# Another order of tasks, maxima items and delays in a fused attention and gated FFN kernel

## The chip, the cores and the metric

The kernel runs on one core of a Trainium2 chip. The metric is the device time of one launch in microseconds, as the median of three runs. The program is one long list of instructions for each engine: TensorE (PE in the profile), VectorE (DVE), ScalarE (ACT), GpSimd (POOL) and SyncE (SP), which here only issues DMAs. Each engine runs its own list strictly in order and waits on semaphores for the others.

## What is computed

```python
xn = layernorm(x)                      # x: (8, 1024, 256)
q, k, v = split(xn @ W_attn + b_attn)  # 16 heads of 16, rope over the heads' axis
att = softmax(causal(q @ k.T / 4))     # per batch and head, 1024 x 1024
s = (att @ v) @ W_proj + b_proj
g = silu((silu(xn @ wg.T) * (xn @ wu.T)) @ wd.T)   # 768 hidden, integer weights / 127
out = x + s * g
```

The tables of the rotation are made for 16 rows and applied along the axis that holds the heads.

## The kernel before

The eight batches run one after the other. The program has a prologue, a body `first` for batch 0, six bodies `mid`, a body `last` and an epilogue. A body has 36 steps (the code says slots): 4 groups of 4 heads, 9 steps each. A step has two halves, a and b. In a half TensorE computes the scores of two heads for one part of the causal triangle (L876, into the three PSUM banks `st`); ScalarE takes the exponential of them (L1133, into `pexp`); GpSimd sets the part above the diagonal to zero in the blocks that touch it (L1618, called the mask here); one step later, in half b, TensorE multiplies `pexp` with the values into `acc` (L927).

The softmax needs the maximum of each row before the exponential. It is computed 12 steps ahead from a second product of the same queries and keys (L903) into the ring, four more PSUM banks, and VectorE reduces it: this is a maxima item. Each half of a step has one item of a kind A, B, E or F out of the table `ITEMS`, two ring banks each. An F item is two plain reductions of 512 columns (L1304). The others touch the diagonal and are masked on the way (L1300): E is one piece of 512 columns a bank, A pieces of 384 and 128, B two pieces of 256. The step that stands at a multiple of nine plus n uses the entry of `ITEMS` that is three further on, so the first entry of the table serves steps 6, 15, 24 and 33.

All other work hangs in these steps as tasks, by the table `TASKS`, which is written out in the code. The names: TX turns the normalised x, QK makes queries and keys, V values, UPG and UPU are the two sides of the FFN's hidden layer, DN its down product, FP the output projection, MT turns the maxima; each of these takes one ring bank. LNS, LNR and LNA are the statistics, the reciprocal roots and the normalising of the layernorm of the next batch; XC copies half of its columns. YS moves unnormalised outputs, YG gathers the sums, YR takes their reciprocal on VectorE, YB stores it, YC spreads it, YN multiplies with it and splits (YH, YL). `("UPU", 1, 3)` is the fourth of six blocks of the second half of the tokens.

TensorE runs a step as: scores, maxima item a, the tasks in the order of the table, scores, maxima item b, the values product. The ring banks are given out in turn in exactly that order, and a use waits until the bank's use four before it is freed. ScalarE and VectorE do the tasks of a half sorted by kind, as `parts_at` lists them (ScalarE: TX, QK, UPG, UPU, V, DN, FP, MT; VectorE: TX, QK, UPG, DN, LNS, MT), not in the table's order. A table `LAG` says how many halves after its step an engine's part of a task stands in that engine's list. SP stores and loads q and k through DRAM; `load_x` brings the x of the batch after the next.

Of the kernel before, what the change touches and what calls it, by code (L numbers as in the profile page):

```python
# [80 lines left out]


TASKS = {
    0: [("DN", 1, 2), ("YS", 3, 0), ("YS", 3, 1)],
    1: [("XC", 0), ("UPG", 0, 0)],
    2: [("V", 0, 1), ("LNS", 0)],
    3: [("XC", 1), ("YG", 1), ("DN", 1, 3)],
    4: [("YR", 1), ("LNS", 1), ("UPG", 0, 1), ("UPU", 0, 0)],
    5: [("LNS", 2), ("UPU", 0, 1), ("YB", 1), ("YC", 1), ("V", 1, 1), ("LNS", 3)],
    6: [("LNR",), ("V", 1, 0)],  # L90
    7: [("UPG", 0, 2), ("YN", 1, 0), ("MT", 1), ("YS", 0, 0), ("YN", 1, 1)],
    8: [("UPU", 0, 2)],
    9: [("LNA", 1), ("UPG", 0, 3)],
    10: [("UPU", 0, 3), ("LNA", 2)],
    11: [("LNA", 5), ("UPG", 0, 4)],
    12: [("FP", 0)],
    13: [("UPU", 0, 4)],
    14: [("YS", 0, 1), ("UPG", 0, 5), ("UPU", 0, 5)],
    15: [("LNA", 6), ("LNA", 3), ("FP", 1), ("LNA", 7), ("FP", 2), ("LNA", 4), ("LNA", 0)],
    16: [("UPG", 1, 0), ("MT", 2)],  # L100
    17: [("YS", 1, 0), ("TX", 0, 1), ("TX", 0, 0), ("TX", 1, 1), ("UPG", 1, 1)],
    18: [("DN", 0, 0)],
    19: [("YS", 1, 1), ("TX", 1, 0), ("QK", 0, 1, 1), ("DN", 0, 1)],
    20: [("DN", 0, 2), ("QK", 0, 0, 1), ("YG", 0), ("QK", 0, 0, 0), ("QK", 0, 1, 0)],
    21: [("DN", 0, 3)],
    22: [("YR", 0), ("UPU", 1, 0), ("UPU", 1, 1)],
    23: [("UPG", 1, 2)],
    24: [("YB", 0), ("QK", 1, 1, 0), ("YC", 0), ("UPU", 1, 2)],
    25: [("FP", 3), ("MT", 3)],
    26: [("UPG", 1, 3), ("UPU", 1, 3)],  # L110
    27: [("YS", 2, 0), ("YN", 0, 0), ("UPG", 1, 4)],
    28: [("YS", 2, 1), ("UPU", 1, 4)],
    29: [("UPG", 1, 5)],
    30: [("YN", 0, 1), ("UPU", 1, 5)],
    31: [("QK", 1, 1, 1), ("QK", 1, 0, 0)],
    32: [("QK", 1, 0, 1)],
    33: [("DN", 1, 0), ("DN", 1, 1)],
    34: [("MT", 0)],
    35: [("V", 0, 0)],
}  # L120
# [1707 lines left out]
```

How the kernel before makes its waits and increments, by code:

```python
def wait(eng, sem, count):  # L375
    if isinstance(count, int) and count <= 0:
        return
    eng.wait_ge(sem, count)
# [183 lines left out]
        def turn(eng, we, wo, cos, sin, tmp, chain, base=0, scale=None):  # L563
            for dst, a, b in ((tmp[0], we, cos), (tmp[1], wo, sin), (tmp[2], wo, cos), (tmp[3], we, sin)):
                if scale is None:
                    last = eng.tensor_tensor(dst, a, b, ALU.mult)
                else:
                    last = eng.scalar_tensor_tensor(out=dst, in0=a, scalar=scale, in1=b, op0=ALU.mult, op1=ALU.mult)
            last.then_inc(chain, 1)
            eng.wait_ge(chain, base + 1)
            eng.tensor_tensor(we, tmp[0], tmp[1], ALU.subtract)
            return eng.tensor_tensor(wo, tmp[2], tmp[3], ALU.add)
# [12 lines left out]
        def rstd_steps(eng, kind, i, pause):  # L586
            base = LN_EACH * ln_number(kind, i) + 2 * TT
            def step(ins, k):
                ins.then_inc(ln_chain, 1)
                if k < 2 + 4 * NEWTON:
                    eng.wait_ge(ln_chain, base + k)
                    if pause is not None:
                        stand(eng, pause)
            eng.wait_ge(ln_chain, base)
            if pause is not None:
                stand(eng, pause)
            step(eng.tensor_scalar(lne[:, :], lnv[:, :, 1], EPS, None, ALU.add), 1)
# [15 lines left out]
        def wait_ready(eng, kind, i, task, name=""):  # L616
            eng.wait_ge(ring_ready[bank(kind, task, name)], use(kind, i, task, name))
```

## Time and profile before

| | |
|---|---|
| median of 3 runs | 1210.34 us (1209.96 to 1210.91) |
| the profiled execution | 1210.59 us |
| its span, first to last instruction | 1208.6 us |
| TensorE, VectorE, ScalarE, GpSimd busy | 93%, 84%, 73%, 63% |
| mean granted clock of TensorE | 0.992 |

The span is what the rows below are counted in; 2 us of the time lie outside it. A duration in a row holds the time until the result is written, so the rows of an engine that never waits overlap; the distance of two starts tells what an instruction takes from its engine. A bracket at a row's end is idle time ahead of it and what ended it.

### The profile page before, as it was taken

The page shows a single profiled execution, that of the slowest core. Times are in us where ns is not written, and L with a number is a line of the kernel's source. Part 1 is how long each engine was busy: PE and PEld are TensorE (multiplying, and loading weights), DVE is VectorE, ACT ScalarE, POOL GpSimd, SP SyncE. Part 2 cuts the span into 40 slices and gives each one's busy share as a digit, 9 for nine tenths or more (in the row PEclk, how much of TensorE's full clock was granted, in tenths as well). Part 3 has the DMA queues.
Part 4 walks back from the last instruction along what each step waited for, and adds up shares of the span by engine and source line. Part 5 has one row for each costly group of instructions (what it writes and reads, how often), then busy time and mean ns, then how long its engine had stood idle before and what let it go on. Part 6 is the DMA issues. An engine that isn't in the chain of part 4 may idle for free.

```text
span 1208.6 us, 27562 instructions
## 1 busy us (share of the span) xinstructions
PE 1125.6 (93%) x9484; PEld 454.8 (38%) x9484; DVE 1012.8 (84%) x3100; ACT 886.5 (73%) x1700; POOL 761.9 (63%) x934
## 2 busy tenths in 40 slices
PE   3789999999999999999999999999999999999996
PEld 2323333434343343434334343343434343343433
DVE  6989989988989888988799878898898887989822
ACT  3358777777877768777777768777787776878774
POOL 3237545495846949298564967469492894747672
PEclk9979999999999999999999999999999999999999
DMA  6250052312442151511624025321525114240201
GB/s 176 71 153 11 11 160 75 88 29 96 105 119 53 30 161 46 137 30 50 165 72 100 20 84 122 120 52 30 144 66 139 30 33 147 72 97 15 62 2 53
DMA packets 69359, 97.49 MB, mean 81 GB/s; under 512 B 16478, under 2 KB 42468, under 8 KB 69220
## 3 DMA queue, kind: packets, MB, share of 16 engines
q1 hardware_dynamic: 69182, 95.72, 29.0%
q8 instruction: 75, 1.23, 0.4%
q14 instruction: 64, 0.52, 0.2%
q10 hardware_dynamic: 38, 0.01, 0.0%
HBM read 52.76 MB, written 34.47 MB: 72 GB/s over the span
## 4 chain that ended last, share of the span: by engine, by line
PE 55%; POOL 20%; DVE 11%; ACT 7%; issue 6%; DMA 1%; POOLq 0%; SPq 0%; DVEq 0%; ACTq 0%
PE ring L936 27%; PE acc L927 12%; PE st L876 8%; PE ring L903 6%; POOL xn L583 5%; POOL hf L1648 4%; DVE ring L1300 3%; POOL pexp L1618 3%; ACT pexp L1133 3%; POOL hT L1657 2%; DVE mx_s L1304 2%; POOL hT L1652 1%; POOL yn L1667 1%; PE ring L946 1%; ACT parts L1175 1%
## 5 line engine op out<-in xcount | busy, mean ns | idle before, releaser
L1133 ACT ACTIVATE pexp<-st 128x512 f32<-128x512 f32 x1152 | 623.7, 598 | 132.1 <-PE st L876 129.6
L1300 DVE CUSTOM_DVE_ANT_0 ring<-ring,tri 128x512 f32<-128x512 f32 (+3 forms) x1024 | 470.6, 522 | 37.3 <-PE ring L903 36.5
L1618 POOL TENSOR_SCALAR_AFFINE_SELECT pexp<-pexp 128x512 f32<-128x512 f32 x256 | 158.0, 635 | 336.2 <-ACT pexp L1133 245.6
L1304 DVE TENSOR_REDUCE mx_s<-ring 128x1 f32<-128x512 f32 x512 | 326.2, 681 | 30.6 <-PE ring L903 29.2
L927 PE MATMUL acc<-pexp,v_pad 128*17 128x512 f32 (+3 forms) x3072 | 304.1, 490 | 16.4 <-POOL pexp L1618 13.8
L903 PE MATMUL ring<-k_st,q_st 56*128 56x512 f16 (+4 forms) x1536 | 239.3, 326 | 17.4 <-DVE g L1372 11.0
L876 PE MATMUL st<-q_st,k_st 58*128 58x512 f16 (+3 forms) x1536 | 234.3, 331 | 3.9 <-ACT pexp L1133 3.4
L876 PEld LDWEIGHTS st<-q_st,k_st 58*128 58x128 f16 x1536 | 61.8, 93 | 276.3 <-ACT pexp L1133 184.3
L1300 DVE DVE_READ_ACCUMULATOR2_ANT mx_s<- 128x1 f32 x1024 | 144.8, 141 | 0.0
L1648 POOL TENSOR_TENSOR hf<-ga,ups 128x512 f32<-128x512 f32 x96 | 121.9, 1274 | 6.9 <-DVE ga L1364 5.3
L927 PEld LDWEIGHTS acc<-pexp,v_pad 128*17 128x17 f32 x3072 | 61.5, 96 | 152.5 <-issue 119.4
L1657 POOL TENSOR_TENSOR hT<-hf,hT 128x512 f16<-128x512 f32 x96 | 111.0, 1160 | 6.7
L903 PEld LDWEIGHTS ring<-k_st,q_st 56*128 56x128 f16 (+1 forms) x1536 | 82.1, 95 | 65.0 <-DVE g L1372 12.9
L936 PE MATMUL ring<-w_dn,hT 128*128 128x256 bf16 x768 | 93.3, 273 | 2.6 <-DVE mx_s L1304 2.3
L936 PE MATMUL ring<-xh,w 128*128 128x512 f16 x256 | 85.1, 387 | 1.1 <-DVE mx_s L1304 0.2
L1364 DVE SCALAR_TENSOR_TENSOR ga<-th,ring 128x512 f32<-128x512 f32 x96 | 66.0, 687 | 19.9 <-ACT th L1190 18.1
L936 PEld LDWEIGHTS ring<-w_dn,hT 128*128 128x128 f16 x768 | 71.6, 98 | 28.6 <-issue 14.8
L1175 ACT ACTIVATE parts<-ring,b_qk 128x512 f16<-128x512 f32 x64 | 44.0, 687 | 45.1 <-PE ring L936 44.9
L936 PE MATMUL ring<-xh,w_ga 128*128 128x512 f16 x192 | 74.2, 386 | 0.7 <-DVE mx_s L1300 0.2
L936 PE MATMUL ring<-xh,w_up 128*128 128x512 f16 x192 | 73.4, 382 | 0.7
L936 PE MATMUL ring<-xl,w_ga 128*128 128x512 f16 x192 | 73.3, 382 | 0.0
L936 PE MATMUL ring<-xl,w_up 128*128 128x512 f16 x192 | 72.8, 379 | 0.0
(151 smaller groups left out, 1322.4 us busy)
## 6 DMA issues: line engine op xcount, KB each, us to landing
parts_scratch<-parts SPq DMA_DIRECT2D x32, 512.0 KB, 3.1
q_st<-parts_scratch SPq DMA_DIRECT2D x62, 192.0 KB, 3.8
k_st<-parts_scratch SPq DMA_DIRECT2D x62, 192.0 KB, 4.4
parts_scratch<-parts SPq DMA_DIRECT2D x32, 256.0 KB, 3.6
xo<-in_x SPq DMA_DIRECT2D x32, 256.0 KB, 3.3
out<-xo SPq DMA_DIRECT2D x32, 256.0 KB, 2.3
xn<-in_x SPq DMA_DIRECT2D x7, 1024.0 KB, 8.0
yn<-yT SPq DMA_DIRECT2D x224, 32.0 KB
```

The lines of the kernel that those rows point to most:

```text
L583: eng.tensor_scalar(xn[:, tt, :], xn[:, tt, :], lnv[:, tt, 0:1], rstd[:, tt:tt + 1], ALU.subtract, ALU.mult).then_inc(xn_ready, 1)
L876: mm = nc.tensor.matmul(st[:, (GH * n + 2 * p + a) % NST, at:at + w], k_st[rows, g, p, kb * P:(kb + 1) * P], q_st[rows, g, p, q0:q0 + w], ...
L903: mm = nc.tensor.matmul(dst[:, at:at + w], q_st[rows, g, p, t * P:(t + 1) * P], k_st[rows, g, p, k0:k0 + w], start=k == 0, stop=k == len(f ...
L927: mm = nc.tensor.matmul(acc[32 * j:32 * j + D + 1, CH - w:CH], v_pad[:, kb, GH * g + j, :], pexp[:, GH * (m % NSET) + j, at:at + w], start ...
L936: mm = nc.tensor.matmul(dst, left, right, start=k == 0, stop=k == len(pairs) - 1)
L1133: nc.scalar.activation(pexp[:, GH * (n % NSET) + j, :], st[:, (GH * n + j) % NST, :], ACT.Exp, scale=1.0 / (QK_SCALE * np.sqrt(D))).then_i ...
L1300: top_ = nc.vector.tensor_tensor_reduce(out=src, in0=src, in1=tri[:, CH - w:CH], scale=1.0, scalar=NEG, op0=ALU.add, op1=ALU.max, accum_ou ...
L1304: top_ = nc.vector.reduce_max(dst, src, AX.X)
L1364: nc.vector.scalar_tensor_tensor(out=ga[:, t[2] % 2, :], in0=th[:, th_buffer(kind, t), :], scalar=1.0, in1=src, op0=ALU.add, op1=ALU.mult) ...
L1618: nc.gpsimd.affine_select(out=t, in_=t, compare_op=ALU.is_ge, fill=0.0, base=0, pattern=[[0, GH], [1, P]], channel_multiplier=-1).then_inc ...
L1648: nc.gpsimd.tensor_tensor(hf[:, u, :], ga[:, u, :], ups[:, u, :], ALU.mult).then_inc(h_full, 1)
L1657: nc.gpsimd.tensor_tensor(hT[:, 1, m, :], hf[:, m % 2, :], hT[:, 0, m, :], ALU.subtract)\
```

## The change

The tables `TASKS`, `ITEMS` and the parts of `LAG` for GpSimd and SP are replaced, and `load_x` stands in step 28 of a body, not in step 21. No instruction is added or removed, and ScalarE's and VectorE's delays stay. A few lines of the diff:

```diff
-ITEMS = ('BF', 'EA', 'FF', 'FF', 'AE', 'AF', 'EA', 'EF', 'BF')
+ITEMS = ('AF', 'FF', 'EF', 'AE', 'FE', 'AF', 'BF', 'EB', 'AF')
...
-    20: [("DN", 0, 2), ("QK", 0, 0, 1), ("YG", 0), ("QK", 0, 0, 0), ("QK", 0, 1, 0)],
+    20: [("QK", 0, 1, 0), ("QK", 0, 0, 0), ("DN", 0, 2)],
...
-LOAD_X = [slot for slot in TASKS if TX_LAST in TASKS[slot]][0] + 2
+LOAD_X = 28
...
-    "gpsimd": {"LNR": 2, "LNA": 0, "XC": 1, "UPU": 2, "HI": 4, "LO": 4, "FP": 2, "FP_G": 2, "FP_X": 4, "YN": 1, "YH": 1, "YL": 2},
-    "sync": {"QK": 2, "MT": 0, "FP": 5, "YS": 0, "YG": 0, "YB": 0, "YC": 1},
+    "gpsimd": {"LNR": 2, "LNA": 0, "XC": 0, "UPU": 3, "HI": 4, "LO": 5, "FP": 2, "FP_G": 3, "FP_X": 5, "YN": 1, "YH": 1, "YL": 4},
+    "sync": {"QK": 6, "MT": 2, "FP": 5, "YS": 2, "YG": 1, "YB": 1, "YC": 3},
```

The tasks of a middle batch that lie on TensorE, by step, before: 0 DN; 1 UPG; 2 V; 3 DN; 4 UPG UPU; 5 UPU V; 6 V; 7 UPG MT; 8 UPU; 9 UPG; 10 UPU; 11 UPG; 12 FP; 13 UPU; 14 UPG UPU; 15 FP FP; 16 UPG MT; 17 TX TX TX UPG; 18 DN; 19 TX QK DN; 20 DN QK QK QK; 21 DN; 22 UPU UPU; 23 UPG; 24 QK UPU; 25 FP MT; 26 UPG UPU; 27 UPG; 28 UPU; 29 UPG; 30 UPU; 31 QK QK; 32 QK; 33 DN DN; 34 MT; 35 V. Now: 0 none; 1 DN; 2 V; 3 DN; 4 UPG UPU; 5 UPG UPU V; 6 V; 7 UPG MT; 8 to 16 as before; 17 TX TX UPG; 18 QK DN; 19 TX TX QK DN; 20 QK QK DN; 21 DN; 22 UPU; 23 UPG UPU; 24 QK UPU; 25 UPG MT; 26 FP; 27 UPU; 28 UPG UPU; 29 UPG; 30 QK UPU; 31 QK; 32 QK; 33 DN; 34 DN MT; 35 V. LNA stand in steps 9, 10, 11 and five times in 15; now in 10, 11, twice in 14, three times in 15, and in 17.

TensorE, step 20 of the fourth batch, from its first maxima to its second, before (L903 are maxima, w_dn is DN, w16 with xh and xl is QK, L876 are scores):

```order
L903 MATMUL ring<-k_st,q_st 128x384 x2
L903 MATMUL ring<-k_st,q_st 128x128 x2
L936 MATMUL ring<-w_dn,hT 128x256 x12
L936 MATMUL ring<-xh,w16 128x512
L936 MATMUL ring<-xl,w16 128x512
L936 MATMUL ring<-xh,w16 128x512 x2
```

and the same place now, with the line numbers of the changed file, one lower:

```order
L935 MATMUL ring<-xl,w16 128x512
L935 MATMUL ring<-xh,w16 128x512
L935 MATMUL ring<-w_dn,hT 128x256 x12
L875 MATMUL st<-q_st,k_st 128x256 x4
L902 MATMUL ring<-k_st,q_st 128x512 x2
```

DN has gone from before the QK tasks to behind them, next to the scores. VectorE's list at this place, before:

```order
L1355 SCALAR_TENSOR_TENSOR parts<-ring,b_qk,parts 128x512 x3
L1372 SCALAR_TENSOR_TENSOR g2<-th,ring 128x256
L1304 TENSOR_REDUCE mx_s<-ring 128x1 x2
```

and now:

```order
L1354 SCALAR_TENSOR_TENSOR parts<-ring,b_qk,parts 128x512 x2
L1371 SCALAR_TENSOR_TENSOR g2<-th,ring 128x256
L1303 TENSOR_REDUCE mx_s<-ring 128x1 x2
```

Here the QK parts stand before DN's g2 in both, with one QK less now. GpSimd from the end of the rstd chain of LNR to the masks of steps 10 and 11, before (yn and ynT are YN, YH and YL, hf and hT are UPU and its halves, xn is LNA):

```order
L608 TENSOR_TENSOR rstd<-rstd,lnt 128x8
L1667 TENSOR_TENSOR yn<-yn 128x512 x2
L1673 CAST ynT<-yn 128x512 x2
L1676 TENSOR_TENSOR ynT<-yn,ynT 128x512 x2
L1648 TENSOR_TENSOR hf<-ga,ups 128x512
L583 TENSOR_SCALAR xn<-xn,lnv,rstd 128x256
L1618 AFFINE_SELECT pexp<-pexp 128x4x128
L1652 CAST hT<-hf 128x512
L1657 TENSOR_TENSOR hT<-hf,hT 128x512
L583 TENSOR_SCALAR xn<-xn,lnv,rstd 128x256
L1618 AFFINE_SELECT pexp<-pexp 128x4x128 x2
```

and now:

```order
L607 TENSOR_TENSOR rstd<-rstd,lnt 128x8
L1656 TENSOR_TENSOR hT<-hf,hT 128x512
L1666 TENSOR_TENSOR yn<-yn 128x512 x2
L1672 CAST ynT<-yn 128x512 x2
L1675 TENSOR_TENSOR ynT<-yn,ynT 128x512 x2
L1647 TENSOR_TENSOR hf<-ga,ups 128x512
L1617 AFFINE_SELECT pexp<-pexp 128x4x128
L1651 CAST hT<-hf 128x512
L582 TENSOR_SCALAR xn<-xn,lnv,rstd 128x256
L1656 TENSOR_TENSOR hT<-hf,hT 128x512
L1617 AFFINE_SELECT pexp<-pexp 128x4x128 x2
```

The LNA ahead of the first mask is gone, and one low part of UPU has come behind the chain from in front of it.

## Rows read from the trace of the kernel before

**Rows 1.** The page: its head, and the busy time of each engine.
```profile
span 1208.6 us, 27562 instructions
...
PE 1125.6 (93%) x9484; PEld 454.8 (38%) x9484; DVE 1012.8 (84%) x3100; ACT 886.5 (73%) x1700; POOL 761.9 (63%) x934
```
**Rows 2.** Windows: stretch, length, busy time and count of each engine, clock, DMA.
```profile
78.00:84.00 6.00, 6.00 (x35) 1.43 (x33) 5.53 (x17) 3.63 (x7) 2.34 (x4) 0.57 1.02 291
...
495.47:637.38 141.91, 135.98 (x1176) 54.70 (x1173) 123.19 (x379) 108.18 (x209) 96.05 (x116) 1.00 0.31 85
```
**Rows 3.** Timeline of PE in step 20: start, length, line, tiles, idle time before.
```profile
578.81 0.38 PE L936 MATMUL ring<-xh,w 128*128 128x512 f16 x1
579.12 0.39 PE L876 MATMUL st<-q_st,k_st 58*128 58x256 f16 x4
581.09 0.39 PE L903 MATMUL ring<-k_st,q_st 56*128 56x512 f16 x2 [1.57 <-DVE g L1372]
```
**Rows 4.** Timeline of DVE in step 20.
```profile
580.62 0.41 DVE L1372 SCALAR_TENSOR_TENSOR g<-th,ring 128x256 f32<-128x256 f32 x1
```
**Rows 5.** Timeline of PE in steps 10 and 11.
```profile
533.68 0.57 PE L903 MATMUL ring<-k_st,q_st 56*128 56x512 f16 x2
535.34 0.62 PE L927 MATMUL acc<-pexp,v_pad 128*17 128x512 f32 x4 [1.09 <-POOL pexp L1618]
...
538.06 0.38 PE L903 MATMUL ring<-k_st,q_st 56*128 56x512 f16 x2
539.54 0.94 PE L927 MATMUL acc<-pexp,v_pad 128*17 128x384 f32 x10 [1.09 <-POOL pexp L1618]
```
**Rows 6.** Timeline of POOL, the rstd chain's start and the mask of step 10.
```profile
521.17 0.25 POOL L600 TENSOR_SCALAR lne<-lnv 128x8 f32<-128x8 f32 x1
...
534.64 0.64 POOL L1618 TENSOR_SCALAR_AFFINE_SELECT pexp<-pexp 128x512 f32<-128x512 f32 x1
```
**Rows 7.** Timeline of POOL and PE, steps 15 to 17.
```profile
554.85 6.03 POOL L583 TENSOR_SCALAR xn<-xn,lnv,rstd 128x256 f32<-128x256 f32 x5
...
560.13 0.63 PE L946 MATMUL ring<-ident,xn 128*128 128x128 f32 x4
560.93 1.14 PE L946 MATMUL ring<-ident,xn 128*128 128x128 f32 x8 [0.17 <-POOL xn L583]
```
**Rows 8.** Timeline of PE in step 34, half b.
```profile
631.87 0.77 PE L876 MATMUL st<-q_st,k_st 58*128 58x512 f16 x2
...
632.89 1.05 PE L927 MATMUL acc<-pexp,v_pad 128*17 128x512 f32 x8
```
**Rows 9.** Timeline of PE and DVE in step 6.
```profile
518.29 0.38 PE L903 MATMUL ring<-k_st,q_st 56*128 56x256 f16 x4
519.36 0.29 PE L936 MATMUL ring<-w,xh 128*128 128x128 f16 x2 [0.69 <-DVE mx_s L1304]
...
518.64 1.26 DVE L1304 TENSOR_REDUCE mx_s<-ring 128x1 f32<-128x512 f32 x2
```
**Rows 10.** Groups by form, 495.47 to 637.38: count, busy us, mean ns, idle before.
```profile
L1304 DVE TENSOR_REDUCE mx_s<-ring 128x1 f32<-128x512 f32 x65 | 41.5, 681 | 4.2 <-PE ring L903 4.1
...
L1300 DVE CUSTOM_DVE_ANT_0 ring<-ring,tri 128x384 f32<-128x384 f32 x32 | 18.5, 579 | 1.7 <-PE ring L903 1.7
```
**Rows 11.** Timeline of SP's queue, steps 22 to 25.
```profile
589.77 0.40 SPq L689 DMA_DIRECT2D xn<-in_x  x1
...
598.08 4.79 SPq L756 DMA_DIRECT2D yn<-inv_scratch  x8
```
**Rows 12.** DMA issues: count, KB each, median us from issue to landing.
```profile
xn<-in_x SPq DMA_DIRECT2D x7, 1024.0 KB, 8.0
...
ysum<-sums_scratch SPq DMA_DIRECT2D x14, 32.0 KB, 2.9
```
**Rows 13.** Timeline of SP's queue and DVE, steps 3 and 5.
```profile
507.06 0.34 SPq L742 DMA_DIRECT2D ysum<-sums_scratch  x1
...
514.62 0.55 DVE L1340 RECIPROCAL yinv<-ysum 128x64 f32<-128x64 f32 x1
```

More of the change, by code:

```diff
@@ L83 @@
 TASKS = {
[L84 to L91, printed above, removed]
+    1: [("DN", 1, 2)],
+    2: [("YS", 3, 0), ("XC", 0), ("XC", 1), ("V", 0, 1), ("LNS", 0), ("YS", 3, 1)],
@@ L92 @@
+    3: [("DN", 1, 3)],
+    4: [("LNS", 1), ("UPG", 0, 0), ("YG", 1), ("YR", 1), ("UPU", 0, 0)],
+    5: [("UPG", 0, 1), ("LNS", 2), ("LNS", 3), ("UPU", 0, 1), ("YB", 1), ("YC", 1), ("V", 1, 0)],
+    6: [("LNR",), ("V", 1, 1)],
+    7: [("UPG", 0, 2), ("YN", 1, 0), ("YN", 1, 1), ("MT", 1)],
     8: [("UPU", 0, 2)],
-    9: [("LNA", 1), ("UPG", 0, 3)],
-    10: [("UPU", 0, 3), ("LNA", 2)],
-    11: [("LNA", 5), ("UPG", 0, 4)],
+    9: [("UPG", 0, 3), ("YS", 0, 0)],
+    10: [("LNA", 7), ("UPU", 0, 3)],
@@ L96 @@
+    11: [("UPG", 0, 4), ("YS", 0, 1), ("LNA", 4)],
     12: [("FP", 0)],
-    13: [("UPU", 0, 4)],
-    14: [("YS", 0, 1), ("UPG", 0, 5), ("UPU", 0, 5)],
-    15: [("LNA", 6), ("LNA", 3), ("FP", 1), ("LNA", 7), ("FP", 2), ("LNA", 4), ("LNA", 0)],
+    13: [("UPU", 0, 4), ("YS", 1, 0)],
+    14: [("UPG", 0, 5), ("LNA", 5), ("UPU", 0, 5), ("LNA", 0)],
+    15: [("FP", 1), ("LNA", 6), ("FP", 2), ("LNA", 1), ("LNA", 2)],
     16: [("UPG", 1, 0), ("MT", 2)],
-    17: [("YS", 1, 0), ("TX", 0, 1), ("TX", 0, 0), ("TX", 1, 1), ("UPG", 1, 1)],
@@ L102 @@
-    18: [("DN", 0, 0)],
-    19: [("YS", 1, 1), ("TX", 1, 0), ("QK", 0, 1, 1), ("DN", 0, 1)],
-    20: [("DN", 0, 2), ("QK", 0, 0, 1), ("YG", 0), ("QK", 0, 0, 0), ("QK", 0, 1, 0)],
[4 rows of a table added]
     21: [("DN", 0, 3)],
[L106 to L112, printed above, removed]
@@ L113 @@
-    29: [("UPG", 1, 5)],
[L114 to L118, printed above, removed]
[1 row of a table added]
+    23: [("UPG", 1, 2), ("UPU", 1, 1)],
+    24: [("YB", 0), ("YC", 0), ("QK", 1, 1, 0), ("UPU", 1, 2)],
+    25: [("UPG", 1, 3), ("MT", 3)],
+    26: [("YN", 0, 0), ("FP", 3)],
+    27: [("UPU", 1, 3)],
+    28: [("UPG", 1, 4), ("UPU", 1, 4)],
+    29: [("UPG", 1, 5)],
[5 rows of a table added]
     35: [("V", 0, 0)],
```

9 rows, old and new, of the table TASKS are left out of this document.

## The prediction

> **What bounds the kernel now.** I read the page first: TensorE is busy 93% of the span, VectorE 84%, the rest less [rows 1]. TensorE's clock is granted in full in the middle batches and falls to 0.57 for some us near the start [rows 2]. That share does not show how much room is left, because the rows give every matmul a modelled tail: matmuls of 512 columns follow each other every 0.22 us while each is listed with 0.38 [rows 3]. So I cut the span at the first score matmul of each batch. One of the six middle batches lasts 141.9 us [rows 2], the other five 141.6 to 142.1; together they are 851 of the 1208.6 us. Then I went through TensorE's rows of the batch that starts at 495.47 and compared each start with the start before it and with the same pair of kinds elsewhere. Scores are followed by their maxima after 0.23 us, maxima by the values product after 0.31. What is longer than that is waiting. Summed over a batch it is about 10 us, so a batch without any wait would take about 131 us. What ended each wait stands in the brackets of its row. The large ones stand at the same places in each middle batch:
>
> - Step 20: the second maxima start at 581.09, 1.97 us after the scores at 579.12, where 0.23 is natural: **1.74 us** [rows 3]. The reason is an order. TensorE runs DN 0 2 before three QK tasks, while ScalarE and VectorE serve QK before DN in a half step. Ring banks are used in turn, four of them: MX, MX, DN, QK, QK, QK, MX. The last needs DN's bank, and VectorE empties that one last, with g at 580.62, after its third QK [rows 4].
> - Steps 10 and 11: the values product waits for the masked pexp: 1.66 and 1.48 us where 0.31 is natural, so **1.35 and 1.17** [rows 5]. GpSimd is late there: from the rstd chain at 521.17 it works without a pause, two YN with their YH and YL, one UPU, one LNA, and comes to the mask at 534.64 [rows 6]. Two more waits of about 0.15 follow in steps 12 and 13, 2.8 us in all.
> - Step 17: the TX tasks wait for GpSimd's five LNA in a row, 6.03 us from 554.85: 0.10 us at 560.13 and 0.36 at 560.93 (four transposes take 0.44), **0.5 us** [rows 7].
> - Step 34: step 34 has almost no TensorE work and an E and an A item for VectorE. Scores at 631.87 to values at 632.89 is 1.02 us for 0.54: **0.5 us** [rows 8].
> - Step 6: V 1 0 waits **0.8 us** (518.29 to 519.36 is 1.07, 0.31 natural) for a bank that VectorE empties late, after two LNS parts; its reductions come at 518.64 [rows 9].
>
> **The change, part by part.** All instructions stay; the count of tasks and items per batch is equal. So the sum is one of waits.
>
> *Step 20.* The step now runs QK, QK, DN, in the order in which ScalarE and VectorE serve them. I went through every step with several tasks: nowhere does TensorE's order now disagree with theirs. The whole 1.74 us goes in the first batch and the six middle ones, since all have these tasks (the last has not): 7 x 1.74 = 12.2 us. One QK has moved to step 18; it takes 1.3 us of TensorE (six matmuls at 0.22), no burst.
>
> *Steps 10 to 13.* Ahead of the mask of step 10 GpSimd now has one LNA less, 1.2 us (five take 6.03 [rows 7]), and the low part of UPU 0 1 has changed places with the rstd chain; both stand ahead of the mask as before, so that is worth nothing. If GpSimd's list of steps 5 to 10 starts when it did, the first wait falls from 1.35 to 0.15. It may start up to 1 us earlier, for steps 0 and 1 have lost an UPG and TensorE comes to step 5 sooner; or UPG 0 1, now one step later, may feed it late and eat the 1.2. Later masks have the same work between them as before. So of 2.8 us between 0.5 and 1.7 stay, at worst all; I take 0.9 and a gain of 1.9 for six batches: 11.4 us. In the first batch there is no YN, and little to gain.
>
> *Step 17.* LNA 5 and 0 stand in step 14, three in 15, LNA 3 in 17, and the two TX tasks that read it in step 19. The first two TX have their inputs 2 us ahead. LNA 3 ends about when TX 0 0 wants it (GpSimd's work up to it ends near 73 us of the batch, TensorE is there near 73), so I keep 0.1 of 0.5: 7 x 0.4 = 2.8 us.
>
> *Step 34 and items.* DN 1 1 comes in front of MT 0 and the items are F and F. VectorE needs about 3.1 us (two F items are four reductions, about 0.6 us each by the pair that takes 1.26 with its tail [rows 9], plus the two tasks) against 3.1 of TensorE: the 0.5 goes, less 0.1: 7 x 0.4 = 2.8 us. Steps 7 and 16 get F, F for E, A as well; their small waits of 0.3 in sum give about 0.3 x 6 = 1.8.
>
> *Step 0* has no TensorE task now. Entering full-height matmuls from the row-split ones costs 0.31 instead of 0.22 us (578.81 to 579.12 [rows 3]), twice a step: 0.2 x 7 = 1.3 us.
>
> *What it costs.* An A item takes VectorE about 1.5 us, F 1.2, E 1.3, B 1.5 (estimates from the means of F's and A's rows and their like [rows 10], less the 0.1 by which such rows overlap). Steps 0 to 5 give VectorE 16.2 us of items where it had 16.0, and step 0 pairs 2.8 us of VectorE with 1.7 of TensorE. VectorE is the last to finish there already (the wait at step 6). I add 0.3 us x 7 = 2. For new short waits elsewhere (UPG 1 1 behind UPU 0 5, V at step 29 behind a mask that comes later, TX 0 0) I set 0.5 x 6 = 3; from below nothing, from above 1.5 a batch.
>
> *x two batches ahead from step 28.* The 1 MB load used to stand before the 32 KB store of inverses: it is issued at 589.77, the store 0.7 us later, and the spreads that wait for that store are issued only at 598.08 [rows 11]. Afterwards the spread comes about 5 us earlier. On the end it is worth nothing: GpSimd reaches YN later anyway, and the scores of step 27, whose row of maxima is queued behind the spreads, hardly wait. The load needs 8 us [rows 12] and is read from step 2 on, over 30 us later: covered. SP's delays of 6 for QK and 2 or 3 for YS, MT, YC do not hold it: SP stands still for data only, and the two stacks of step 24 are issued as soon as QK is done.
>
> Sum: -12.2 -11.4 -2.8 -2.8 -1.8 -1.3 + 2 + 3 = -27.3. The profiled execution took 1210.59 us, 2 more than its span, and 0.25 above the median of the runs: 1210.59 - 27.3 = 1183.3, **1183 us**.
>
> **Rivals.**
> - *Only step 20 pays.* Every wait removed elsewhere gives GpSimd and VectorE less time, and they are busy 96 and 123 of its 142 us [rows 2]; VectorE's list in steps 0 to 6 is full. For it: the wait at step 6 stays. Against: the masks' lateness is a matter of what stands before them. It gives 1210.6 - 12.2 = 1198.
> - *The gather blocks VectorE: slower.* Now all eight stack loads, the two xo loads and both YS stand in front of YG in SP's queue, and YG and the reciprocal YR are in the same half step 4b; VectorE waits in line on it with all maxima behind. Before, the gather was issued at 507.06, 7.6 us before the reciprocal at 514.62 [rows 13]; it lands after 2.9 us [rows 12], which leaves 4.7 us. If YG is issued over 4.7 us later, each further us is one of VectorE and of TensorE behind it. The moves of y are small and now queue behind eight loads of the stacks. At 4.7 us plus the 4.5 us that a middle batch gains, so from YG 9 us late, it decides; 10 us late, 5.3 over for six batches, gives 1183 + 32 = 1215. Against: the stack loads only change places with YS 3 1, which waits for step 1. The Trainium skill's page "DMA: Bandwidth & Descriptors", section "Queues, rings and completion order", says that descriptors are taken in ring order on each DMA engine, which speaks for this rival. By that rule a late YG follows, and the trace agrees in the inverse store behind the x load.
> - *More than I count.* All of steps 10 to 17 and half of step 6 go: 5 us more over six batches and more in the first, whose start runs at that lower clock for some us [rows 2]: 1163 to 1173.
> - *Nothing.* The waits move on to VectorE's late maxima: 1210.
>
> **How the numbers follow.** The forecast's own range: downward no new waits (-5), 0.5 us kept at the masks (-2.4) and none in steps 17 and 34 (-2.1), 1173; upward 1.7 us kept (+4.8) and 1.5 us a batch of new waits (+6), 1194. It has 0.70. More: 0.08. Only step 20: 0.12. Nothing: 0.04. Slower: 0.06. The range takes in the forecast, half of the case above it in gain and the step-20 case with 5 us of spread: 1168 to 1203. The rest, some 0.18, is out. A measurement here tells 0.2%, 2.4 us, from no change. Faster 0.89 (the first three, less a little), same 0.04, slower 0.07.
>
> **What would show it.** Middle batches of about 137.4 us. In step 20 the second maxima 0.23 us after the scores. The wait of the values product for masks in steps 10 and 11 under 1 us in sum, the mask of step 10 about 38.0 to 39 us after the batch's start (it was 39.2). No wait at TX in step 17. The wait at V in step 6 still 0.7 to 0.9. The reciprocal with no idle time before it. It is wrong if VectorE idles at L1339, if the order in SP's queue delays the stacks for step 24 or the row of maxima for step 0, or if waits for VectorE's maxima grow by over 3 us a batch.

## The result, and the profile after

The changed kernel takes 1180.2 us (median of 4, 1179.2 to 1180.5) where the kernel before, timed beside it, takes 1210.6 (1209.96 to 1211.26). The ratio is 0.9747, 95% interval 0.9730 to 0.9764. The forecast was 1183 with a range of 1168 to 1203: 27.3 us off were forecast and 30.4 came.

The page of the kernel after, its head and the busy time of each engine:

```profile
span 1177.2 us, 27562 instructions
...
PE 1119.9 (95%) x9484; PEld 454.4 (39%) x9484; DVE 1011.4 (86%) x3100; ACT 886.4 (75%) x1700; POOL 761.5 (65%) x934
```

The work is the same, instruction for instruction, and so is VectorE's and GpSimd's busy time [rows 1]; only the span is 31.4 us shorter. The fourth and the third batch, each cut from its first score matmul to the next batch's:

```profile
484.32:621.94 137.62, 135.25 (x1177) 54.65 (x1174) 123.25 (x379) 108.15 (x209) 96.03 (x116) 1.00 0.31 87
346.23:484.32 138.09, 135.05 (x1177) 54.58 (x1174) 123.09 (x379) 108.16 (x209) 96.11 (x116) 1.00 0.32 87
```

The other four middle batches last 136.1 to 137.2 (before: 141.6 to 142.1 each [rows 2]); these two are the longest: the third waits 1.7 us at step 24, the fourth 0.4 there and 0.9 more in steps 27 to 29. Step 24 is taken up below. By place, from the same cuts in both traces: prologue +0.8, first batch -2.8, six middle batches 850.7 to 821.8, so -28.8, last batch and epilogue -0.6; the sum is -31.4.

The waits, place by place. For every pair of consecutive groups on TensorE (scores, maxima, values, tasks) I took the usual shortest distance of such a pair in the trace before, and called what is longer a wait. The mean per middle batch, in us, by steps; small entries up to about 0.2 are also differences between shapes. The kernels below the second line are those of the experiments. A pair that the trace before does not have is not counted; one such pair, maxima to values in step 31, is long in e15_qk2, so its entry for steps 30 to 33 is that of the changed kernel, 0.53, and the 4.64 us that these steps last longer (19.79 for 15.15). Where TensorE's clock falls behind a wait, the slower matmuls are in the numbers too.

```
run               0    1-4    5-6    7-9  10-13  14-16     17  18-19     20  21-23     24  25-29  30-33  34-35  total
before         0.07   0.94   0.85   0.51   3.01   0.38   0.65   0.19   1.78   0.25   0.31   0.42   0.53   0.56  10.46
after          0.70   0.15   1.04   0.28   0.66   0.26   0.40   0.21   0.04   0.10   0.59   0.49   0.53   0.08   5.53
e1_step20      0.07   0.94   0.85   0.51   3.01   0.38   0.66   0.19   0.05   0.24   0.31   0.59   0.53   0.56   8.88
e2_dn_first    0.70   0.15   1.03   0.29   0.67   0.26   0.41   0.20   1.78   0.10   0.22   0.52   0.53   0.08   6.94
e6_one_lna     0.07   0.93   0.85   0.51   1.79   0.38   1.63   0.21   1.78   0.24   0.31   0.42   0.53   0.56  10.21
e9_lna_and_tx  0.07   0.93   0.85   0.51   1.80   0.38   0.50   5.01   1.78   0.24   0.30   0.36   0.53   0.56  13.84
e12 (+ delays) 0.07   0.95   0.85   0.51   1.60   0.38   0.49   1.00   1.79   0.25   0.30   0.36   0.64   0.56   9.76
e5g_pool_lag   0.70   0.15   1.04   0.28   0.87   0.26   0.40   3.49   0.04   0.10   0.10   0.50   0.53   0.08   8.56
e15_qk2        0.70   0.15   1.03   0.28   0.66   0.26   0.40   0.21   0.04   7.27   1.59   0.33   5.17   0.08  18.17
e4_load21      0.70   0.15   1.04   0.28   0.67   0.26   0.40   0.20   0.04   0.10   3.01   0.41   0.53   0.08   7.88
e7_items       0.71   0.30   0.65   0.51   0.97   0.38   0.50   0.39   0.04   0.46   0.24   0.51   0.53   0.08   6.26
e14_dn0        0.07   1.35   1.04   0.28   0.66   0.26   0.40   0.21   0.04   0.10   0.55   0.50   0.53   0.08   6.07
```

Two places carry most of the gain, 1.7 us in step 20 and 2.35 in steps 10 to 13. Step 20 in the timeline of PE after, which answers to [rows 3]:

```profile
565.13 0.39 PE L875 MATMUL st<-q_st,k_st 58*128 58x256 f16 x4
565.36 0.38 PE L902 MATMUL ring<-k_st,q_st 56*128 56x512 f16 x2
```

The second maxima stand 0.23 us behind the scores, where 1.97 lay before, and have no bracket. Step 11, where the values product waited for the mask [rows 5]:

```profile
525.35 0.38 PE L902 MATMUL ring<-k_st,q_st 56*128 56x512 f16 x2
525.80 1.06 PE L926 MATMUL acc<-pexp,v_pad 128*17 128x384 f32 x16
```

The distance is 0.45 us where 0.31 is natural, 0.14 of wait for 1.17; in step 10 it is 0.07 for 1.35. The timelines of POOL and PE in the same batch, the mask of step 10 and LNA 3, and the TX of step 19 that reads it:

```profile
521.02 0.64 POOL L1617 TENSOR_SCALAR_AFFINE_SELECT pexp<-pexp 128x512 f32<-128x512 f32 x1
...
553.77 1.22 POOL L582 TENSOR_SCALAR xn<-xn,lnv,rstd 128x256 f32<-128x256 f32 x1
```
```profile
555.42 1.09 PE L945 MATMUL ring<-ident,xn 128*128 128x128 f32 x8
```

The mask of step 10 comes 36.7 us after the batch's start (521.02 less 484.32), earlier than the 38 to 39 forecast; it was 39.2 [rows 2, 6]. LNA 3 ends at 554.99, only 0.4 us before its TX starts. That narrow margin is the key to the experiments below.

### The profile page after: what moved, and what is told of

Read it like the earlier page. It is cut to its first block, busy times and chain, and to the rows that moved or that the text cites. A ratio compares the mean times of both kernels' runs of the same rounds, so it can differ in the third digit from the quotient of the medians.

```text
span 1177.2 us, 27562 instructions
## 1 busy us (share of the span) xinstructions
PE 1119.9 (95%) x9484; PEld 454.4 (39%) x9484; DVE 1011.4 (86%) x3100; ACT 886.4 (75%) x1700; POOL 761.5 (65%) x934
## 4 chain that ended last, share of the span: by engine, by line
PE 60%; POOL 14%; DVE 8%; issue 6%; DMA 5%; ACT 4%; SPq 2%; POOLq 0%; DVEq 0%; ACTq 0%
PE ring L935 26%; PE acc L926 15%; PE st L875 10%; PE ring L902 7%; POOL xn L582 3%; DVE ring L1299 2%; POOL hf L1647 2%; ACT pexp L1132 2%; POOL pexp L1617 2%; DVE mx_s L1303 1%; DMA k_st<-parts_scratch 1%; POOL yn L1666 1%; DMA parts_scratch<-parts 1%; POOL so L1686 1%; POOL hT L1656 1%
## 5 line engine op out<-in xcount | busy, mean ns | idle before, releaser
L902 PE MATMUL ring<-k_st,q_st 56*128 56x512 f16 (+5 forms) x1536 | 235.9, 326 | 9.5 <-ACT ups L1180 3.3
L935 PE MATMUL ring<-xh,w 128*128 128x512 f16 x256 | 87.7, 388 | 0.3
```

The source lines that it names most:

```text
L902: mm = nc.tensor.matmul(dst[:, at:at + w], q_st[rows, g, p, t * P:(t + 1) * P], k_st[rows, g, p, k0:k0 + w], start=k == 0, stop=k == len(f ...
L935: mm = nc.tensor.matmul(dst, left, right, start=k == 0, stop=k == len(pairs) - 1)
```

## The experiments

Each was timed in five rounds beside the kernel before, which took 1209.7 to 1210.4 us. The changed kernel's 1180.2 is the other end of the scale. Each says what it is an edit of.

**Step 20 alone** (an edit of the kernel before):

```diff
-    20: [("DN", 0, 2), ("QK", 0, 0, 1), ("YG", 0), ("QK", 0, 0, 0), ("QK", 0, 1, 0)],
+    20: [("QK", 0, 0, 1), ("YG", 0), ("QK", 0, 0, 0), ("QK", 0, 1, 0), ("DN", 0, 2)],
```

> The kernel before with one edit: in step 20 DN 0 2 stands last, behind the three QK tasks; nothing is moved between steps. The prediction's term: the 1.74 us of step 20 goes in seven batches, 12.2 us, so about 1198.4, ratio 0.990, and the second maxima start 0.23 us after the scores. Rival (the wait moves): DN's hand-over comes later in the half step, VectorE's last hand-over is then late for the first maxima of step 21 or for the value product behind it, and less than half is kept: 1204 to 1210.

Measured: 1198.9 us, ratio 0.9902 (0.9885 to 0.9919). Its step 20 in the timeline of PE:

```profile
573.27 0.39 PE L876 MATMUL st<-q_st,k_st 58*128 58x256 f16 x4
573.50 0.38 PE L903 MATMUL ring<-k_st,q_st 56*128 56x512 f16 x2
```

The distance is 0.23, the whole wait of 1.7 us is gone (table, column 20), and hardly anything comes up elsewhere: 11.4 us of the 12.2. The order within one step is shown to be the cause, and the wait does not move on.

**The same the other way** (an edit of the changed kernel):

```diff
-    20: [("QK", 0, 1, 0), ("QK", 0, 0, 0), ("DN", 0, 2)],
+    20: [("DN", 0, 2), ("QK", 0, 1, 0), ("QK", 0, 0, 0)],
```

> The changed kernel with DN 0 2 first in step 20 again, ahead of its two QK tasks. Four ring banks are used in turn, so the second of the two maxima groups of half b needs DN's bank, which VectorE empties last. If the order is what counts, a wait of 1 to 1.7 us is back there in seven batches: 1187 to 1192. Rival (three QK tasks in one step were the trouble, and the one moved to step 18 is what helped): under 0.3 us a batch, 1180 to 1182.

Measured: 1187.6 us, ratio 0.9813 (0.9795 to 0.9831), 7.4 more than the changed kernel. The timeline of PE, first and second head of the second maxima, which are two uses of the ring here:

```profile
570.27 0.38 PE L902 MATMUL ring<-k_st,q_st 56*128 56x512 f16 x1
572.00 0.39 PE L902 MATMUL ring<-k_st,q_st 56*128 56x512 f16 x1 [1.35 <-DVE g L1371]
```

With one QK less in the step the second head's use still falls on DN's bank, and waits for the same g. In the trace the wait is 1.7 again, and 0.4 comes back at step 24, whose loads then have more time.

**One LNA moved behind the masks** (an edit of the kernel before):

```diff
-    9: [("LNA", 1), ("UPG", 0, 3)],
+    9: [("UPG", 0, 3)],
-    14: [("YS", 0, 1), ("UPG", 0, 5), ("UPU", 0, 5)],
+    14: [("YS", 0, 1), ("UPG", 0, 5), ("LNA", 1), ("UPU", 0, 5)],
```

> The kernel before with one edit: LNA 1 stands in step 14 and not in step 9, so GpSimd has 1.2 us less to do ahead of the masks of steps 10 and 11, and as much more between them and the TX tasks of step 17. The prediction's account of the masks (their lateness is only a matter of what stands ahead of them): the wait of step 10 falls by 1.2 us in six batches and the rest stays, 7.2 us, about 1203.4. Rival (GpSimd has no pause between the masks of step 4 and the last LNA, so its work up to the first TX task sets the time of step 17, wherever it stands): the mask wait falls by 1.2 us, the wait at TX in step 17 grows from 0.5 to about 1.7, and the time is 1210.5, within 1.5.

Measured: 1210.05 us, ratio 0.9997 (0.9986 to 1.0008): nothing. The timelines of PE, steps 11 and 17, and of POOL, the five LNA of step 15:

```profile
540.33 0.94 PE L927 MATMUL acc<-pexp,v_pad 128*17 128x384 f32 x10 [1.04 <-POOL pexp L1618]
...
561.65 0.66 PE L946 MATMUL ring<-ident,xn 128*128 128x128 f32 x4 [0.76 <-POOL xn L583]
562.85 1.09 PE L946 MATMUL ring<-ident,xn 128*128 128x128 f32 x8 [0.55 <-POOL xn L583]
```
```profile
556.76 6.04 POOL L583 TENSOR_SCALAR xn<-xn,lnv,rstd 128x256 f32<-128x256 f32 x5
```

Steps 10 to 13 lose 1.2 us of wait and step 17 gains 1.0: what the mask gives, TX takes back. GpSimd's timeline before has no idle time between the masks of step 4 at 513.57 and the last of the five LNA, but for the bubbles inside the rstd chain. So its whole list up to there is one block of about 47 us, and TensorE is held to it at the next point where it needs a result. The prediction's account of the masks by itself falls here.

**The places of LNA and TX taken over** (an edit of the kernel before; FP, YS and all others stay):

```diff
-    9: [("LNA", 1), ("UPG", 0, 3)],
-    10: [("UPU", 0, 3), ("LNA", 2)],
-    11: [("LNA", 5), ("UPG", 0, 4)],
+    9: [("UPG", 0, 3)],
+    10: [("LNA", 7), ("UPU", 0, 3)],
+    11: [("UPG", 0, 4), ("LNA", 4)],
-    14: [("YS", 0, 1), ("UPG", 0, 5), ("UPU", 0, 5)],
-    15: [("LNA", 6), ("LNA", 3), ("FP", 1), ("LNA", 7), ("FP", 2), ("LNA", 4), ("LNA", 0)],
+    14: [("YS", 0, 1), ("UPG", 0, 5), ("LNA", 5), ("UPU", 0, 5), ("LNA", 0)],
+    15: [("FP", 1), ("LNA", 6), ("FP", 2), ("LNA", 1), ("LNA", 2)],
-    17: [("YS", 1, 0), ("TX", 0, 1), ("TX", 0, 0), ("TX", 1, 1), ("UPG", 1, 1)],
+    17: [("YS", 1, 0), ("TX", 1, 1), ("LNA", 3), ("TX", 0, 1), ("UPG", 1, 1)],
-    19: [("YS", 1, 1), ("TX", 1, 0), ("QK", 0, 1, 1), ("DN", 0, 1)],
+    19: [("TX", 0, 0), ("YS", 1, 1), ("TX", 1, 0), ("QK", 0, 1, 1), ("DN", 0, 1)],
```

> The kernel before with the places of the eight LNA and of the TX tasks taken from the changed kernel: no LNA in step 9, LNA 7 and 4 in 10 and 11, 5 and 0 in 14, 6, 1 and 2 in 15, LNA 3 behind TX 1 1 in step 17, TX 0 0 in step 19; all else as before. By the prediction's terms it is worth 1.2 to 1.9 us at the masks and 0.4 at TX per batch: 9.6 to 14.2 us, 1196 to 1201. By the rival of the run with one LNA moved, the gain needs the TX tasks' later deadline and is that whole sum here and nothing there; TX in step 17 then has no wait, and the masks of steps 10 to 13 keep about 1.2 of 2.8 us, since two halves of UPU and YL still stand ahead of them. If only the order of the LNA within GpSimd's list counted, this run would gain no more than the run with one LNA moved.

Measured: 1229.4 us, ratio 1.0146 (1.0125 to 1.0167): 19 us slower than before, which neither theory had. The timelines of POOL and PE at steps 17 to 19, and the window behind the wait:

```profile
567.05 2.50 POOL L1687 TENSOR_TENSOR so<-so,b_pr 128x512 f32<-128x512 f32 x2
...
574.46 1.21 POOL L583 TENSOR_SCALAR xn<-xn,lnv,rstd 128x256 f32<-128x256 f32 x1
```
```profile
575.73 1.09 PE L946 MATMUL ring<-ident,xn 128*128 128x128 f32 x8 [3.22 <-POOL xn L583]
...
577.89 0.63 PE L936 MATMUL ring<-xl,w 128*128 128x512 f16 x1
578.32 0.63 PE L936 MATMUL ring<-xh,w 128*128 128x512 f16 x1
```
```profile
576.00:581.00 5.00, 5.00 (x26) 2.96 (x24) 2.04 (x3) 1.77 (x3) 0.27 (x1) 0.66 0.49 133
```

LNA 3 stands in GpSimd's list behind the whole of FP 1 and FP 2 (bias, gate and residual, six operations from 567.05 to 574.46, 7.4 us) and is late by 3.2 us for TX 0 0. Then the clock's granted share is 0.66 over the next 5 us: matmuls of 512 columns follow each other after 0.43 us in place of 0.22, the rate of the lower of the two levels. Both together are the 5.0 of column 18-19. The gain at the masks (1.2) is there again and is swallowed.

**The same with GpSimd's new delays**. The edit is the last one and

```diff
-    "gpsimd": {"LNR": 2, "LNA": 0, "XC": 1, "UPU": 2, "HI": 4, "LO": 4, "FP": 2, "FP_G": 2, "FP_X": 4, "YN": 1, "YH": 1, "YL": 2},
+    "gpsimd": {"LNR": 2, "LNA": 0, "XC": 0, "UPU": 3, "HI": 4, "LO": 5, "FP": 2, "FP_G": 3, "FP_X": 5, "YN": 1, "YH": 1, "YL": 4},
```

> The kernel before with the places of LNA and TX of the changed kernel (the run that came out at 1229) and with GpSimd's new row of delays as well. The 2.5 us of residual additions stand behind LNA 3 now, so that it ends near 72.0 us of the batch and not near 74.5, where TensorE comes to it near 71.3: the wait of 4.8 us of step 19 falls to about 0.7, 1.7 of it being the clock that no longer falls. With 1.2 us of the mask wait of step 10 gone as before: about 1204. Rival (the wait of step 19 has to do with the place of TX or QK on TensorE, not with GpSimd's list): it stays near 1229.

Measured: 1206.1 us, ratio 0.9974 (0.9963 to 0.9986), 23 less than without the delays. PE at step 19, where LNA 3 ends at 565.26:

```profile
564.83 0.38 PE L903 MATMUL ring<-k_st,q_st 56*128 56x384 f16 x4
565.32 1.09 PE L946 MATMUL ring<-ident,xn 128*128 128x128 f32 x8
```

TX waits 0.2 us (0.49 for 0.31), and 0.6 to 0.8 stand in step 18, where DN waits for its hT. The wait of step 19 was GpSimd's list, as the theory has it, and 1206 is close to the 1204 reckoned.

**GpSimd's delays taken out of the changed kernel**: the reverse of the last diff.

> The changed kernel with GpSimd's row of delays as it was before (UPU 2, LO 4, XC 1, FP_G 2, FP_X 4, YL 2), all else changed. Theory from the run with LNA and TX moved (GpSimd works without a pause from the masks of step 4 to LNA 3, and what stands ahead of LNA 3 sets when TX 0 0 of step 19 can start): FP_X at 4 puts both residual additions of FP 1 and 2 ahead of LNA 3, 2.5 us; LNA 3 ends 0.4 us ahead of its TX now, so TX waits about 2.1 us in the six middle batches, and up to 1.7 more where TensorE's clock falls after the wait: 1193 to 1203. Rival (the delays only say where things stand and are worth nothing, as the prediction took them to be): 1180, within 1.5.

Measured: 1197.8 us, ratio 0.9904 (0.9887 to 0.9921), 17.6 us more than the changed kernel. PE at step 19:

```profile
562.60 1.09 PE L945 MATMUL ring<-ident,xn 128*128 128x128 f32 x8 [2.08 <-POOL xn L582]
```

2.1 us, as reckoned from 2.5 of work and 0.4 of margin. In the six middle batches TensorE stands idle there for 1.9 to 2.2 us, and in four of them 1.5 to 1.7 us of slower matmuls come behind it. So GpSimd's row of delays carries more than the order in step 20. The run changes the whole row; the wait is of the size of the two additions of FP_X, which the row puts ahead of LNA 3, but FP_X was not tried by itself.

**SP's delays taken out of the changed kernel**:

```diff
-    "sync": {"QK": 6, "MT": 2, "FP": 5, "YS": 2, "YG": 1, "YB": 1, "YC": 3},
+    "sync": {"QK": 2, "MT": 0, "FP": 5, "YS": 0, "YG": 0, "YB": 0, "YC": 1},
```

> The changed kernel with SP's row of delays as it was before (QK 2, MT 0, YS 0, YG 0, YB 1, YC 1), all else changed. Theory: the waits of 0.3 to 1.7 us for the stacks at step 24 (in batches 2, 3, 5 and 6), of 0.5 at step 27 and 29 in batch 3, 4.3 us in all, come from QK's parts being stored 6 half steps late, close ahead of the loads that step 24 needs; with 2 they go: 1176. Rival (they come from the traffic on the DMA engines, or another transfer is late once QK's go first): 1179 to 1182, with the waits at other places.

Measured: 1271.8 us, ratio 1.0517 (1.0499 to 1.0536): 92 us slower than the changed kernel, where 4 faster was expected. (YB goes back to 0 in this run as well; the expectation has it as 1.) It was the largest miss of the study, and this run settled it:

**Only QK's delay on SP** (an edit of the changed kernel, `"QK": 6` to `"QK": 2`):

> The changed kernel with one number of SP's row put back, QK 2 in place of 6. Theory from the run with the whole row (1272): SP then issues the four stores of parts, waits for their receipt, issues eight loads, and only then comes to the gather YG; its sums land behind the place of the reciprocal, VectorE stands there for 6 us and TensorE behind it. That one number makes the whole loss: 1268 to 1275. Rival (YS, YC or YG in the row had a share): under 1250.

Measured: 1269.6 us, ratio 1.0490 (1.0471 to 1.0509). One number makes nearly all of it. SP's queue, VectorE, PE and windows, steps 20 to 24 of its fourth batch:

```profile
601.94 0.64 SPq L675 DMA_DIRECT2D parts_scratch<-parts  x1
607.13 0.80 SPq L636 DMA_DIRECT2D q_st<-parts_scratch  x2
...
610.89 0.35 SPq L741 DMA_DIRECT2D ysum<-sums_scratch  x1
```
```profile
617.39 0.55 DVE L1339 RECIPROCAL yinv<-ysum 128x64 f32<-128x64 f32 x1 [7.81 <-DMA ysum<-sums_scratch]
```
```profile
618.77 0.60 PE L902 MATMUL ring<-k_st,q_st 56*128 56x512 f16 x1 [6.68 <-DVE mx_s L1299]
```
```profile
615.00:618.00 3.00, 0.00 (x0) 0.00 (x0) 0.61 (x2) 0.00 (x0) 1.76 (x2) 0.58 0.34 54
618.00:621.00 3.00, 2.08 (x10) 0.53 (x14) 3.00 (x11) 0.00 (x0) 0.00 (x0) 0.50 0.11 33
```

And SP's queue in the changed kernel at the same place:

```profile
564.05 0.34 SPq L741 DMA_DIRECT2D ysum<-sums_scratch  x1
...
566.27 0.69 SPq L675 DMA_DIRECT2D parts_scratch<-parts  x1
571.86 0.80 SPq L636 DMA_DIRECT2D q_st<-parts_scratch  x2
```

With QK at 2, SP issues the four stores, issues the first load 5.2 us after the last of them, since it has to wait for their receipt, then the rest of eight loads of 192 KB, and only then the 32 KB gather. The gather's sums, which land after 1.8 us in the changed kernel's stretch, land there after 6.4 (DMA rows of the two stretches). The reciprocal waits 7.8 us, every maxima reduction behind it too, TensorE 6.7, and its clock then stands at 0.50.

That is about two thirds of the loss. A middle batch lasts 12.6 us longer than in the changed kernel; 8.2 of them lie in steps 23 and 24, and 4.6 in steps 31 and 32, where the same number does it a second time. SP's queue, ScalarE and PE there:

```profile
648.84 0.43 SPq L675 DMA_DIRECT2D parts_scratch<-parts  x1
...
650.10 2.47 SPq L734 DMA_DIRECT2D yn<-yT  x4
```
```profile
654.03 0.60 ACT L1142 ACTIVATE yT<-acc 128x512 f32<-128x512 f32 x1 [3.35 <-DMA yn<-yT]
```
```profile
654.77 1.48 PE L926 MATMUL acc<-pexp,v_pad 128*17 128x512 f32 x16 [3.34 <-ACT yT L1142]
```

The stores of the parts of step 30 stand ahead of YS 2 0 and hold it back until those parts are made; ScalarE cannot empty `acc` into `yT` before YS 2 0 has moved the old `yT` away, and TensorE cannot start the next values product. In the changed kernel YS 2 0 goes first, its four moves of y from 597.42, and the stores follow at 603.27.

The first of the two is the mechanism of the prediction's slower rival. It is not in step 4, where the prediction looked for it, but in step 22, and the delay of 6, called harmless in the text, is what keeps the gather ahead. The Trainium skill's page "DMA: Bandwidth & Descriptors", section "Two DMAs through the same engine are not ordered", says that descriptors within one queue of one DMA engine start in order; the landing of 6.4 for 1.8 us agrees.

**The x load's place, in the kernel before** (`LOAD_X` 28 in place of 21) and **in the changed kernel** (21 in place of 28):

> The kernel before with LOAD_X at 28 in place of 21 and nothing else. The spreads of the inverses, which wait behind the x load now, should be issued some 5 us earlier. By the prediction's term that is worth nothing: 1210, within 1.5. Rival (the row of maxima that is queued behind the spreads makes the scores of step 27 wait, and stacks at step 24 share the DMA engines with the load): up to 1 us a batch, 1204 to 1208.

> The changed kernel with LOAD_X at 21, where the load stood before; there it is issued between YS 1 1 and the gather YG, ahead of the stores of QK's parts. If the transfers behind it are late by the 5 us that the load takes, the gather still lands ahead of its reciprocal (7 us of room), but the stacks of step 24, which have no room in half of the batches, are late by 3 to 5 us in six batches: 1198 to 1210. Rival (the load shares the DMA engines and holds nobody up): 1180 to 1183.

Measured: 1209.9 us for the first, ratio 0.9996 (0.9988 to 1.0005), and 1192.7 for the second, ratio 0.9853 (0.9839 to 0.9866). SP's queue before had the spreads at 598.08 [rows 11]; in the first run they come at 594.45, counted from the batch's start 3.0 us earlier and not 5, and that is worth nothing:

```profile
594.45 3.55 SPq L756 DMA_DIRECT2D yn<-inv_scratch  x8
```

In the second the load stands ahead of the stores of the parts, and TensorE waits for the stacks at step 24:

```profile
570.42 0.51 SPq L688 DMA_DIRECT2D xn<-in_x  x1
...
573.67 1.17 SPq L675 DMA_DIRECT2D parts_scratch<-parts  x1
581.13 0.80 SPq L636 DMA_DIRECT2D q_st<-parts_scratch  x2
```
```profile
587.07 0.54 PE L902 MATMUL ring<-k_st,q_st 56*128 56x384 f16 x4 [1.74 <-DMA k_st<-parts_scratch]
```

The loads follow the last store by 7.5 us where it was 5.6, and step 24 waits 3.0 us a batch for 0.6. The same move is worth nothing in the one table and 12.5 us in the other.

**The items** (the changed kernel with the nine items of before):

> The changed kernel with the maxima items of before (BF EA FF FF AE AF EA EF BF). By the prediction's terms the new items are worth about 0.3 to 0.5 us at step 34 in seven batches and 0.3 at steps 7 and 16 in six, less their cost of up to 0.3 in steps 0 to 6: 1182 to 1185. Rival (items are worth nothing without TensorE waiting for VectorE there, DN 1 1 in step 34 has taken the wait away alone): 1179 to 1181.

Measured: 1180.8 us, ratio 0.9757 (0.9743 to 0.9770), so 0.6 us more. Steps 34 and 35 stay at 0.08 with the old items: DN 1 1 alone removed that wait. By the table steps 1 to 23 wait 1.45 us a batch more, without 5 and 6, which wait 0.4 less, as does step 24; 0.7 in sum, where the cuts show 0.4 a batch and the time 0.6 for the whole kernel. What the items are worth is less than can be told here.

**DN back in step 0** (an edit of the changed kernel):

```diff
-    1: [("DN", 1, 2)],
+    0: [("DN", 1, 2)],
```

> The changed kernel with DN 1 2 in step 0 and none in step 1. Step 0's waits of 0.5 (maxima) and 0.2 us (values) come from items A and E, 2.8 us of VectorE beside 1.7 of TensorE; with a task there they should go. Theory (VectorE is the later engine through steps 0 to 6, so its total counts and not the place): the wait comes back in step 1 or 5 and the time is 1179 to 1182. Rival (the wait is local to step 0): 0.7 us in seven batches, 1175 to 1177.

Measured: 1182.6 us, ratio 0.9771 (0.9757 to 0.9784). The 0.63 of step 0 goes and 1.2 comes in step 1. The engine that I had named is wrong. The timelines of PE and ACT, step 0 of the changed kernel:

```profile
484.32 0.39 PE L875 MATMUL st<-q_st,k_st 58*128 58x512 f16 x2
...
484.77 0.38 PE L875 MATMUL st<-q_st,k_st 58*128 58x512 f16 x1
485.45 0.39 PE L875 MATMUL st<-q_st,k_st 58*128 58x512 f16 x1 [0.31 <-ACT pexp L1132]
```
```profile
484.80 2.06 ACT L1132 ACTIVATE pexp<-st 128x512 f32<-128x512 f32 x4 [0.33 <-PE st L875]
```

Without a task between them the two halves' scores are 0.45 us apart, and the fourth of them needs a bank of `st` that ScalarE frees at its exponentials' pace of about 0.5 us. It is not VectorE's maxima but ScalarE that a step without a task exposes. In step 1, where ScalarE has an evacuation of `acc` on top, it costs twice as much.

## Why the prediction was right, by its steps

The total was forecast within 3.1 us, and part of that is luck. Step 20 and step 34 came as forecast and masks and TX together near it (15.6 for 14.2), but the account of the masks does not hold by itself, and two misses nearly cancel: step 0 is 5.1 us worse than forecast, and the places under "what it costs" are 6.9 better (1.9 gained where 5 were set as a loss).

- *Step 20, 12.2 us:* right in cause, place and size. 1.74 us of wait went in all seven batches; alone it measured 11.4.
- *Steps 10 to 13, 11.4 us, and step 17, 2.8 us:* the trace shows 2.35 x 6 = 14.1 and 0.25 x 6 = 1.5 (forecast 0.4 x 7), so the sum was right. The step "later masks have the same work between them as before", with the masks and TX costed as two separate things, was wrong in kind. Moving an LNA behind the masks alone is worth 0 us. It pays since three things come together: TX 0 0, which reads LNA 3, is due two steps later, the two residual additions (FP_X at 5) stand behind LNA 3, and GpSimd's block starts 16.9 us after the batch's start and not 18.1 (its masks of step 4 at 501.25 and 513.57), where steps 0 and 1 have lost an UPG. The prediction named that last one as possible, with 1 us, and did not count it. The traces bear it out. The list of GpSimd from the masks of step 4 on is the same, operation for operation, in the run with LNA, TX and delays (first line) and in the changed kernel (second line):

```profile
511.51 1.22 POOL L1618 TENSOR_SCALAR_AFFINE_SELECT pexp<-pexp 128x512 f32<-128x512 f32 x2 [3.15 <-ACT pexp L1133]
```
```profile
501.25 1.22 POOL L1617 TENSOR_SCALAR_AFFINE_SELECT pexp<-pexp 128x512 f32<-128x512 f32 x2 [3.01 <-ACT pexp L1132]
```

  From there to the start of LNA 3 (564.04 and 553.77) both take 52.5 us, so only the start differs, 18.1 and 16.9 us into the batch. With it the masks' wait goes from 1.60 to 0.66, and that of steps 17 to 19 from 1.49 to 0.61, 1.8 us a batch together, in part because of the QK that now stands in step 18 ahead of DN; that run gained only 3.6 us. The sentence "LNA 3 ends about when TX 0 0 wants it" held: the margin is 0.4 us.
- *Step 34 and the items, 2.8 + 1.8 us:* 0.48 x 6 = 2.9 us in steps 34 and 35, by DN 1 1 alone. Steps 7 to 9, 14 to 16 and 21 to 23 lost 0.5 a batch, 3 us; with the old items the table has 0.51, 0.38 and 0.46 there again, so they are the items', but the time of that run is only 0.6 us more.
- *Step 0, a gain of 1.3 us:* wrong sign. It lost 0.63 x 6 = 3.8 us: the step counted a switch of matmul shapes and not what the task had covered, ScalarE's exponentials.
- *What it costs, 2 + 3 us:* steps 1 to 4 gained 0.8 a batch, 4.7 us, where a loss was set (four waits of 0.15 to 0.26 went, two of them for VectorE's maxima by their brackets; no run takes the moves there apart); steps 5 and 6 lost 0.2, 1.1 us, and the wait at V in step 6, given as a sign with 0.7 to 0.9, is 0.45 now, with 0.46 new in step 5; step 24 lost 0.3, 1.7 us, and it was not among the costs. That last one is the prediction's own warning come true, "if the order in SP's queue delays the stacks for step 24". In the third batch, the longest:

```profile
428.14 0.34 SPq L741 DMA_DIRECT2D ysum<-sums_scratch  x1
428.68 0.34 SPq L673 DMA_DIRECT2D parts_scratch<-parts  x1
...
436.47 0.82 SPq L636 DMA_DIRECT2D k_st<-parts_scratch  x2
```
```profile
439.31 0.39 PE L875 MATMUL st<-q_st,k_st 58*128 58x512 f16 x2
441.19 0.39 PE L902 MATMUL ring<-k_st,q_st 56*128 56x384 f16 x4 [1.49 <-DMA k_st<-parts_scratch]
```

  The stores can only follow the gather, which itself waits for y, and their loads then land 1.5 us after TensorE has come for them, in this batch; in two of the six it costs nothing. It is the price of keeping the gather first, and a small one beside the 89 us of the other order.
- *x two batches ahead:* worth nothing in the kernel before, as said, but the changed kernel loses 12.5 us without it. And the sentence that SP's delays hold nothing up was wrong. The delay does not make SP wait, it sets what stands behind what, and here one number is worth 89 us.
- *The rivals:* "only step 20 pays" is what the run with step 20 alone gives, 1199 (1198 was forecast for it), and it is not what the change gives. "The gather blocks VectorE" did not come: the reciprocal at 573.46 has no bracket, nor has any of the 14. "Nothing" and "more than I count" did not come either.

The middle batches were forecast at 137.4 us (the terms of the sum give 4.1 us a batch and not 4.5, so 137.7) and last 136.1 to 138.1, 137.0 in the mean. The step-by-step differences over the six middle batches add up to -29.6 us (10.46 less 5.53, by six), against -28.8 by the cuts.

What stays open: why GpSimd's block starts 1.2 us earlier. No run had the moved UPG by themselves. Ahead of the masks of step 4 TensorE now has one UPG less, which takes 0.97 us, waits 0.79 less in steps 1 to 4 and 0.63 more in step 0; that makes 1.1, but it is a sum and not a run. Nor was a version tried that keeps the gather first and gets the parts' stores earlier; none of the runs beats the changed kernel.

## What to carry to other kernels

An engine whose list runs without a pause over many steps is one block: moving work inside it only moves the wait to the next consumer, and gains come from what is taken out from ahead of the last deadline, or from a later deadline. So before an order is judged, mark the stretches in which each engine has no idle time, and sum what stands ahead of each point where another engine needs it. In a queue that takes its entries in order, ask of every entry which small, urgent transfer it is put ahead of; and where units of a ring are given out in one engine's order, let the engines that free them work in the same order.

A step without a task is not free time: ask which engine's work the task was hiding.
